# Short products of late projections in two row halves and two banks, biases added at the eviction

## What is computed

```python
q = (layernorm(x) @ Wq + bq)                 # 4 x 256 tokens, 256 columns
k = (ctx_768 @ Wk + bk)                      # 4 x 4096 tokens, 256 columns
v = (ctx_768 @ Wv + bv)
attn = softmax(clip(q k^T * 16**-0.5, -10000, 10000))     # per head
x = x + (attn v) @ Wo + bo
x = x + self_attention(layernorm(x))         # causal, with layernorms of q and k
x = x + slot_ffn(layernorm(x))               # routing to 64 slots, top 8
```

## Time and profile before

| | |
|---|---|
| median of 3 runs | 1238.16 us (1236.31 to 1242.47) |
| the profiled execution | 1239.52 us |
| its span in the profile | 1237.7 us |
| mean granted TensorE clock | 0.989 |
| first score unit of the main loop | 113.43 us |
| groups 1 to 7, 9 and 10 | 60.74 us each |
| group 11, with three jobs | 55.85 us |
| groups 12 to 14, without jobs | 47.2 to 48.5 us |
| end of the last group | about 1030 us |

### The profile page before, as it was taken

One profiled execution on the slowest core, in us unless ns is written; L12 is line 12 of the kernel. 1 busy time (PEld: TensorE's weight loads), 2 busy tenths in 40 slices (PEclk: granted clock), 3 DMA queues, 4 the chain that ended last, 5 costly groups with the idle time before them and its releaser, 6 DMA issues.

```text
span 1237.7 us, 26185 instructions
## 1 busy us (share of the span) xinstructions
PE 1180.8 (95%) x10272; PEld 713.7 (58%) x10276; DVE 849.5 (69%) x1554; ACT 729.3 (59%) x1328; POOL 163.7 (13%) x199
## 2 busy tenths in 40 slices
PE   7998999999999999999999999999999997979986
PEld 6775665656665656665556566555454445546654
DVE  4776777777777777777777777778888604493453
ACT  2224676767676767676667676767777873404331
POOL 5353121111111111111111111001000004000010
PEclk9898999999999999999999999999999999999999
DMA  7655435343434343444334443322443000000001
GB/s 204 189 150 150 111 105 124 104 115 100 113 101 112 104 109 106 110 109 112 106 109 110 114 109 104 87 65 73 115 137 82 15 1 1 0 2 2 2 1 35
DMA packets 153330, 111.34 MB, mean 90 GB/s; under 512 B 18566, under 2 KB 152407, under 8 KB 153177
## 3 DMA queue, kind: packets, MB, share of 16 engines
q1 hardware_dynamic: 146167, 103.18, 31.1%
q10 hardware_dynamic: 7010, 6.23, 1.8%
HBM read 81.41 MB, written 27.79 MB: 88 GB/s over the span
## 4 chain that ended last, share of the span: by engine, by line
PE 88%; DVE 5%; ACT 3%; issue 2%; DMA 1%; SPq 1%; POOL 0%; DVEq 0%; POOLq 0%; ACTq 0%
PE acc L1468 20%; PE st L1427 20%; PE mx L1415 17%; PE kps L1375 8%; PE kps L1384 7%; PE st L1384 2%; DVE kst L1191 2%; ACT prob L881 2%; PE setB L1715 1%; PE acc L1375 1%; PE kps L1415 1%; PE st L1635 1%; PE setB L1724 1%; PE misc L1441 1%; PE misc L1479 1%
## 5 line engine op out<-in xcount | busy, mean ns | idle before, releaser
L972 DVE TENSOR_REDUCE mxp<-mx 128x1 f32<-128x512 f32 x959 | 626.6, 686 | 221.7 <-PE mx L1415 218.5
L1427 PE MATMUL st<-qst,kst 99*128 99x256 bf16 x2048 | 389.2, 274 | 4.0 <-issue 1.9
L796 ACT ACTIVATE prob<-st 128x512 f32<-128x512 f32 x512 | 288.8, 598 | 135.4 <-PE st L1427 134.5
L1415 PE MATMUL mx<-kst,qst 96*128 96x512 bf16 x959 | 364.1, 382 | 4.5 <-DMA qst<-qscr 3.7
L1427 PEld LDWEIGHTS st<-qst,kst 99*128 99x128 bf16 x2048 | 177.0, 98 | 215.3 <-issue 49.4
L796 ACT ACTIVATE xn<-st 128x512 f32<-128x512 f32 x256 | 144.7, 597 | 90.8 <-PE st L1427 90.8
L796 ACT ACTIVATE xnT<-st 128x512 f32<-128x512 f32 x256 | 150.3, 598 | 51.0 <-PE st L1427 48.3
L1468 PE MATMUL acc<-prob,v_raw 128*17 128x256 f32 x2048 | 135.4, 382 | 2.3 <-ACT prob L796 1.3
L527 POOL CAST kraw<-kraw 128x512 bf16<-128x512 f32 x50 | 30.6, 611 | 600.0 <-DVE kraw L933 600.0
L1415 PEld LDWEIGHTS mx<-kst,qst 96*128 96x128 bf16 x959 | 92.5, 96 | 25.6 <-DVE mxp L972 6.4
L1384 PE MATMUL kps<-wv,ctx 128*128 128x256 f32 (+1 forms) x376 | 96.8, 379 | 0.0
(11 more groups left out here) (382 smaller groups left out, 1033.9 us busy)
## 6 DMA issues: line engine op xcount, KB each, us to landing
kst<-kscr SPq DMA_DIRECT2D x120, 192.0 KB, 2.9
kst<-kscr SPq DMA_DIRECT2D x360, 64.0 KB, 2.7
kscr<-kraw SPq DMA_DIRECT2D x100, 192.0 KB, 2.6
ctx<-in_ctxT SPq DMA_DIRECT2D x93, 128.0 KB, 2.4
ctx<-in_ctxT SPq DMA_DIRECT2D x93, 64.0 KB, 2.3
kscr<-prob SPq DMA_DIRECT2D x16, 192.0 KB, 3.5
kscr<-o_sb SPq DMA_DIRECT2D x12, 192.0 KB, 3.7
qscr<-v_raw SPq DMA_DIRECT2D x12, 128.0 KB, 2.0
```

Of the source, the lines that this page charges most:

```text
L796: act.activation(exps(n), st[n % 3][:, :], ACT.Exp).then_inc(exp_done, 1)
L972: dve.reduce_max(at, bank_of_max(n)[:, :], AX.X).then_inc(max_red, 1)
L1415: pe.matmul(bank_of_max(n)[:, :], qst[0:96, 4 * (q % 3) + j, qt * P:(qt + 1) * P], kst[0:96, j, at:at + 512], start=True, stop=True).then_ ...
L1427: mm = pe.matmul(st[n % 3][:, h * T:(h + 1) * T], kst[0:99, j, at:at + P], qst[0:99, 4 * (q % 3) + j, :], start=True, stop=True)
```

## The change

Weights and late context chunks have their last 64 rows twice, in the partitions 0 to 63 and 64 to 127. misc and kps become the two banks of one tensor mk. A late job writes its two halves into the two banks: the 128-row product of half 1 (kps) at its first step, that of half 0 (misc) at its second, and at its third both 64-row products, one from the lower rows and one from the upper. The steps of job i are 9+6i, 11+6i and 13+6i (9, 12 and 13 for job 0). ScalarE evicts one step after the third, VectorE two steps after it. The early chunks stay in one bank and in one row half, with 64 rows in place of 65 in the second product.

The biases leave the products: K's is added by the two evictions (per half: ScalarE with a bias, VectorE with a scalar_tensor_tensor), V's after the attention, where the attended rows are turned (softmax weights add up to 1). The rows of ones and their memsets go. take_sums and normalise stand one and two steps earlier. SP's write_k and load_ctx follow the new steps, and load_ctx writes the 64 rows twice.

```diff
         acc = psum("acc")
-        misc = psum("misc")
-        kps = psum("kps")
+        mk = psum("mk", 2)
+        misc, kps = mk[:, 0, :], mk[:, 1, :]
...
-        def bank_of_k(c):
-            return (kps, acc)[c % 2] if c < KLEAD else kps
+        def bank_of_k(c, g):
+            return (kps, acc)[c % 2][:, g * CH:(g + 1) * CH] if c < KLEAD else mk[:, g, 0:CH]
...
+        def job_at(i):
+            return (9, 12, 13) if i == 0 else (9 + 6 * i, 11 + 6 * i, 13 + 6 * i)
+        def steps_of(i):
+            return (13 + 6 * i - 1) // 8, (18 + 6 * i - 1) // 8
...
             def load_ctx(slot, c):
                 sp.dma_start(ctx4[:, slot, 0, :], a["ctxT"][c, 0:P, :]).then_inc(ctx_in[slot], 16)
-                sp.dma_start(ctx4[0:C2, slot, 1, :], a["ctxT"][c, P:C, :]).then_inc(ctx_in[slot], 16)
+                sp.dma_start(ctx4[:, slot, 1, :], both(a["ctxT"][c, P:C, :])).then_inc(ctx_in[slot], 16)
...
-            sp.dma_start(wk[0:C2, 1, :], a["L0_xattn_Wk"][P:C, :]).then_inc(w_in, 16)
-            sp.dma_start(wk[C2:C2 + 1, 1, :], a["L0_xattn_bk"].rearrange("(o n) -> o n", o=1)).then_inc(w_in, 16)
+            sp.dma_start(wk[:, 1, :], both(a["L0_xattn_Wk"][P:C, :])).then_inc(w_in, 16)
+            with nc.allow_non_contiguous_dma("256 biases onto partitions"):
+                sp.dma_start(bk[:, :], a["L0_xattn_bk"].rearrange("(g p) -> p g", p=P)).then_inc(w_in, 16)
...
-                    if k % 2 == 1 and k_job(q, k - 1) is not None:
-                        write_k(k_job(q, k - 1))
-                    c = k_job(q, k)
-                    if c is not None and c + 2 < NCH:
-                        sp.wait_ge(k_ps, c + 1)
-                        load_ctx(c % 2, c + 2)
-                    c = v_job(q, k)
-                    if c is not None and c + 2 < NCH:
-                        sp.wait_ge(v_ps, c + 1)
-                        load_ctx(2 + c % 2, c + 2)
+                    for i in range(8):
+                        c = k_job(q, i)
+                        if c is not None and steps_of(i)[1] == k:
+                            write_k(c)
+                        if c is not None and c + 2 < NCH and steps_of(i)[0] == k:
+                            sp.wait_ge(k_ps, c + 1)
+                            load_ctx(c % 2, c + 2)
+                        c = v_job(q, i)
+                        if c is not None and c + 2 < NCH and steps_of(i)[0] == k:
+                            sp.wait_ge(v_ps, c + 1)
+                            load_ctx(2 + c % 2, c + 2)
...
-            pool.wait_ge(consts, 3)
-            pool.memset(early[C2:C2 + 1, 3:16, CH:2 * CH], 1.0).then_inc(consts, 1)
-            pool.wait_ge(consts, 4)
-            pool.memset(ctx4[C2:C2 + 1, :, 1, :], 1.0).then_inc(consts, 1)
-            pool.wait_ge(consts, 5)
...
-                pool.wait_ge(k_r, c + 1)
+                pool.wait_ge(k_r, 2 * (c + 1))
...
+                    if k == 1:
+                        act.activation(to, (st[0], st[2])[n][:, :], ACT.Identity, bias=bv[:, 0:1]).then_inc(xnT_act, 1)
+                    else:
+                        act.activation(to, (st[0], st[2])[n][:, :], ACT.Copy).then_inc(xnT_act, 1)
...
-                act.activation(parts_of(c)[:, :, 0, :], bank_of_k(c)[:, :].rearrange("p (g t) -> p g t", g=2),
-                               ACT.Copy).then_inc(k_1, 1)
+                for g in range(2):
+                    act.activation(parts_of(c)[:, g, 0, :], bank_of_k(c, g), ACT.Identity,
+                                   bias=bk[:, g:g + 1]).then_inc(k_1, 1)
...
-                if t % 8 == 5:
-                    c = k_job(q, t // 8)
-                    if c is not None:
-                        k_first(c)
-                    c = v_job(q, t // 8)
-                    if c is not None:
-                        v_copy(kps, c)
+                for i in range(8):
+                    if t == job_at(i)[2] + 1:
+                        if k_job(q, i) is not None:
+                            k_first(k_job(q, i))
+                        if v_job(q, i) is not None:
+                            v_copy(mk[:, :, 0:CH], v_job(q, i))
...
-                dve.wait_ge(k_1, c + 1)
                 wait(dve, k_3, c - 1)
-                dve.tensor_tensor(kres[:, c % 2, :, :], bank_of_k(c)[:, :].rearrange("p (g t) -> p g t", g=2),
-                                  parts_of(c)[:, :, 0, :], ALU.subtract).then_inc(k_r, 1)
+                for g in range(2):
+                    dve.wait_ge(k_1, 2 * c + (g + 1 if c >= KLEAD else 2))
+                    dve.scalar_tensor_tensor(kres[:, c % 2, g, :], bank_of_k(c, g), bk[:, g:g + 1],
+                                             parts_of(c)[:, g, 0, :], ALU.add, ALU.subtract).then_inc(k_r, 1)
...
+                if t == 9 and q > 0:
+                    take_sums(q - 1)
                 if t == 10 and q > 0:
-                    take_sums(q - 1)
-                if t == 12 and q > 0:
                     normalise(q - 1)
-                if t % 8 == 6:
-                    c = k_job(q, t // 8)
-                    if c is not None:
-                        k_rest(c)
+                for i in range(8):
+                    if t == job_at(i)[2] + 2 and k_job(q, i) is not None:
+                        k_rest(k_job(q, i))
...
-                    rows = P if n == 0 else C2 + 1
+                    rows = P if n == 0 else C2
...
+            def full_k(c, g):
+                pe.matmul(mk[:, g, 0:CH], wk[:, 0, g * P:(g + 1) * P], ctx4[:, c % 2, 0, :], start=True, stop=False)
+            def full_v(c, t):
+                pe.matmul(mk[:, t, 0:D], ctx4[:, 2 + c % 2, 0, t * P:(t + 1) * P], wv[:, 0, :], start=True, stop=False)
+            def rest_k(c):
+                for g in range(2):
+                    rows = slice(C2 * g, C2 * g + C2)
+                    mm = pe.matmul(mk[:, g, 0:CH], wk[rows, 1, g * P:(g + 1) * P], ctx4[rows, c % 2, 1, :],
+                                   start=False, stop=True)
+                mm.then_inc(k_ps, 1)
+            def rest_v(c):
+                for t in range(2):
+                    rows = slice(C2 * t, C2 * t + C2)
+                    mm = pe.matmul(mk[:, t, 0:D], ctx4[rows, 2 + c % 2, 1, t * P:(t + 1) * P], wv[rows, 1, :],
+                                   start=False, stop=True)
+                mm.then_inc(v_ps, 1)
+            def job_step(q, t):
+                for i in range(8):
+                    if t not in job_at(i):
+                        continue
+                    step = job_at(i).index(t)
+                    c = k_job(q, i)
+                    if c is not None:
+                        if step == 0:
+                            pe.wait_ge(*k_ctx_sem(c))
+                            pe.wait_ge(k_r, 2 * c)
+                            pe.wait_ge(v_out, VLEAD + 4 * q + i // 2)
+                            full_k(c, 1)
+                        elif step == 1:
+                            if i == 0:
+                                wait(pe, head_out, 2 * q)
+                                pe.wait_ge(low_set, 2 * q + 2)
+                            full_k(c, 0)
+                        else:
+                            rest_k(c)
+                    c = v_job(q, i)
+                    if c is not None:
+                        if step == 0:
+                            pe.wait_ge(*v_ctx_sem(c))
+                            pe.wait_ge(k_r, 2 * min(KLEAD + 4 * q + i // 2 + 1, NCH))
+                            pe.wait_ge(v_out, c)
+                            full_v(c, 1)
+                        elif step == 1:
+                            full_v(c, 0)
+                        else:
+                            rest_v(c)
             def early_k(c, g):
                 if g == 0:
                     pe.wait_ge(*ctx_sem(c))
-                    wait(pe, k_r, c - 1)
-                project_k(bank_of_k(c), ctx_of(c), g)
...
+                    if q > 0:
+                        pe.wait_ge(v_out, min(VLEAD + 4 * q, NCH))
...
-                if t % 8 in (0, 4):
-                    g = t % 8 // 4
-                    c = k_job(q, k)
-                    if c is not None:
-                        if g == 0:
-                            pe.wait_ge(*k_ctx_sem(c))
-                            pe.wait_ge(k_r, c)
-                            pe.wait_ge(v_out, VLEAD + 4 * q + k // 2)
-                        project_k(kps, ctx4[:, c % 2, :, :], g)
-                    c = v_job(q, k)
-                    if c is not None:
-                        if g == 0:
-                            pe.wait_ge(*v_ctx_sem(c))
-                            pe.wait_ge(k_r, min(KLEAD + 4 * q + k // 2 + 1, NCH))
-                            pe.wait_ge(v_out, c)
-                        project_v(kps, ctx4[:, 2 + c % 2, :, :], g)
+                job_step(q, t)
```

(24 more changed lines are left out.)

45 lines of the change are left out of this document (25 added, 20 removed).

## The result

| | before | after |
|---|---|---|
| median | 1239.85 us (4 runs, 1236.31 to 1242.47) | 1409.05 us (4 runs, 1400.71 to 1414.11) |
| the profiled execution | 1239.52 us | 1413.03 us |
| mean granted TensorE clock | 0.989 | 0.971 |
| first score unit | 113.43 us | 140.76 us |
| usual query group | 60.74 us | 71.40 us, or 73.0 and 74.6 with one and two falls of the clock |

The ratio is 1.1341 (95% interval 1.1302 to 1.1381). The span grew by 173.5 us: 27.3 ahead of the first score, 143.8 in groups 0 to 10, and 2.4 in all that follows.

A forecast was written before the change was run, and what follows sets the result against it. TensorE, busy for 95% of the span, was taken as the bound. The terms -11.8 + 16.8 + 1.0 + 77.9 + 26.4 + 17.4 = +127.7 took 1239.5 to 1367.2; less 1.4 for the median, 1366 us, range 1310 to 1420.

The forecast's parts named there:

- What bounds it: In the main loop TensorE is full, so any saving or new wait there shows in the time.
- Rival 1: The bank waits don't show because the step that releases a bank was misread: 1262 us, 7%.
- The pair: In 91 late jobs, two side-by-side 64-row products take 0.74 instead of 0.87: 0.13 saved each, -11.8 us.
- Rivals 3 and 4: 3: switching form is free and evictions end in time, 1199, 3%; 4: short products run in turn, 1405, 5%.
- The early short rows: Early chunks' 64-row products cost 0.30 a half, 16.8 us in the first loop; the start ahead of it +1.0.
- The K wait: After a K job, the V job's first product waits for VectorE's k_rest: 1.77 each, 44 times, 77.9 us.
- The V wait: After a V job, the next K job's first product waits for ScalarE's copy: 0.80 each, 33 times, 26.4 us.
- The empty stretch: Steps 56 to 8 hold no jobs, losing 0.85 at group starts and 0.81 at ends: 17.4 us.
- The clock: A fall to 1.2 GHz after one in four waits, +27 us, within the range but not in the sum.
- Rival 2: After waits of 1.8 us the clock falls to 1.2 GHz, after each K job: 110 more, 1476 us, 7%.

The follow-up runs named there:

- e10_rest_first: After, with VectorE's part of the K eviction ahead of that step's maximum reduction instead of behind it: 1327.36 us.
- e3_one_half: After, with both short products of a late job read from rows 0 to 63: 1488.19 us, with a first loop at half clock.
- e8_all: e7_aligned with early second products at 65 rows, doubled weights loaded later, K bias on its own semaphore, shift's second turn at step 62: 1247.34 us.
- e1_v_later: After, with the first two steps of the V jobs moved from 15+6i and 17+6i to 17+6i and 18+6i: 1345.96 us.
- e7_aligned: After, with job steps moved so that every K pair stands at a step divisible by 4, beside the values group: 1277.10 us.
- e5_bias_apart: After, with the K bias DMA on its own semaphore, so TensorE's first product no longer waits for it: 1405.36 us.
- e2_both_later: After, with the steps of jobs 1 to 7 at 11+6i, 12+6i and 13+6i: 1374.35 us, with a first loop at half clock.
- e12_both_again: The kernel of e2_both_later timed again, unchanged: 1333.71, 1334.82, 1336.04 and once 1372.8 us.
- e4_before_early64: The kernel before, with only the early chunks' second products at 64 rows instead of 65, leaving out those chunks' biases: 1257.52 us.

## Why the prediction came out as it did

The direction and all but 43 us of the 169 were forecast, by the mechanism that the runs confirm. Step by step:

**What bounds it.** Right. The waits of TensorE showed in the time: 1.27 less of each K wait (e10_rest_first) made a group 5.1 shorter, four times as much. Rival 1, in which they don't show, is out.

**The pair.** Right: 0.73 against 0.87, so 0.14 for my 0.13; the halves overlap (e3_one_half) and the switches eat two thirds of what that saves. Rivals 3 and 4 are out.

**The early short rows.** Right in size: 17.0 us alone in the kernel before, against my 16.8 in the loop and 7.2 less hidden 3.7 ahead of it. From first maximum to first score it was 14.5 for my 14.2. I saw that 65 rows run without a gap and 64 don't, in two rows of the trace. The Trainium skill, TensorEngine Tiling (Array Packing), section Key Properties, has the drain at a change of tiling mode. The trace agrees: a 64-row product between larger ones costs 0.30.

**"The bias DMAs change from a row to 256 scattered elements: within 1 us either way."** Of the bias by itself this holds: 3.8 for 3.50 us to landing, where nothing doubled is ahead of it (e8_all). What failed is that this was all I priced. I didn't count the weight rows that are written twice: they land at 10.36 us where a single copy lands at 6.07, and they hold the bias behind them until 12.0 to 13.4. I looked at which engine removed its work and not at how long the new transfers take. The first maximum product came 12.8 late where I had 3.6: 3.2 for the short rows, 7.0 for these loads, and 2.6 because the slow passes of the start lasted 13.3 us in the profiled execution, for 7.0 before. That is 9 us. The 2.6 are chance of the execution: e10_rest_first has the same start and 7.6 us of slow passes. Over the seven executions with this start, the miss is 5 to 10.

**The K wait.** Right in place and in kind, 1.86 for 1.77. The two subtractions took 0.87 where I chose 0.76 between 0.68 and 0.85 (one is 0.47), the signal 0.09 where I had 0.14, and the product behind the wait took 0.08 more than usual (0.51 for 0.43) where I had 0.07. 44 x 0.09 = 4 us. My note that less than 1.2 a job isn't possible while VectorE reduces first holds too: with the order turned it was 0.59.

**The V wait.** 0.84 for 0.80, 1.3 us in all.

**The empty stretch.** 10.66 a group, less 4 x 1.86 and 3 x 0.84, plus 8 x 0.14, leaves 1.8 for my 1.66: 2 us over 11 groups. The steps show it directly, and that the two parts were off in opposite ways: steps 0 to 7 take 6.79 for pieces of 6.12, so 0.67 where I had 0.85, and steps 56 to 63 take 7.26 for 6.12, so 1.14 where I had 0.81.

**The clock.** This is the term that I had as a possibility (one fall in four, +27, in the range but not in the sum) and that came: 16 falls, 26 us. Rival 2 was right in its mechanism and wrong in its share of the waits, one in three and not every one; and my counterexample, 29 us at full clock with gaps of about 1 us, had shorter gaps. That the waits cause the falls is shown by three schedules: with gaps of 0.4 (e1_v_later), 0.3 (e10_rest_first) or none (e7_aligned) the falls behind them are gone, while e3_one_half and e5_bias_apart, which keep the gaps of 1.6, have 16 falls each like after. That my range held them is in part luck: no row of before showed how often a fall follows a wait.

Together 9 + 4 + 1 + 2 + 26 = 42. They are read from the profiled execution, which at 1413.03 is 4 above the median and 46 above the 1367.2 that I had for it. The other 4 are 2.4 behind the groups and 1.8 in group 2, a single wait ahead of a values group; e1, e2, e3, e7, e10 and e12 have it as well (1.5 to 1.9 us), before doesn't, and its cause is open. Open too: why a fall follows one wait and not the next, how long the slow passes at the start last, and what keeps the first loop at half clock in some executions.

## What to carry to other kernels

A second accumulation bank that is shared by consecutive jobs has to be priced by the evictions: find the step in which each engine gives the bank back, by its own program order, and put the next writer behind it, under the longest thing that TensorE has to do anyway. Here the whole gain of the row pairs was at most 13 us (91 x 0.14), and one reduction that VectorE did first cost 56 in waits and 24 in clock. And count the start: a transfer that gates the first product costs all of its latency. Here the doubled load had 8.07 us of it for 3.78, and what stood behind it in the queue was late as well.

## What was not expected of the hardware

- A lone product of 64 rows costs 0.30 us more than one of 65 (step 1.38 for 1.09, e4_before_early64), with the same columns and the same result size.
- The load that writes 64 weight rows twice landed 8.07 us after its issue (e5_bias_apart), the single copy in its place 3.78 (e8_all). A DMA of 256 scattered elements of 4 bytes behind it took 9.0 to 10.5 us, and 3.8 behind the single copy. From 12.5 to 16 us the DMA engines were busy for a share of 0.14 in after and in e5_bias_apart, and for 0.79 and 0.87 in before and e8_all, which have no doubled load there.
- Waits of TensorE that leave it idle for 1.6 us bring the clock down to 1.2 GHz for 3.4 us about every third time (15 of 44 in after); idle times of 0.3 to 0.6 us didn't (e1_v_later, e10_rest_first).
- In the profiles of e2_both_later and e3_one_half the first loop stayed at 0.50 for 85 us, with TensorE busy all through (85.30 of 85.30 in e2_both_later), so here a full engine didn't get its clock back soon. One of the four executions of e12_both_again is as long (1372.8 us).
